# Attention stage of a graph network: VectorE's wide products read a bank operand, GpSimd adds the own rows, three sum banks

## The chip, the cores and the metric

One core of one Trainium2 chip. The metric is the device time of the whole kernel in microseconds (us); an execution's own time stands beside the span that the hardware profiler gives for it.

## The reference

Four layers of a graph network on 50,000 nodes with 64 features and 50,000 edges, sorted by their destination node. Each layer is `x = x + layer(relu(layernorm(x)))`: a convolution, a mean, an attention layer and a layer with two edge types that runs three times. The change touches the attention layer, with 4 heads:

```python
src, dst = edges + one loop per node
m = leaky_relu(x_l[src] + x_r[dst] + e_emb, 0.2)      # (edges, 4, 64)
alpha = einsum('ehf,hf->eh', m, att)
amax = segment_max(alpha, dst); ex = exp(alpha - amax[dst])
denom = segment_sum(ex, dst)
out = segment_sum(x_l[src] * (ex / (denom[dst] + 1e-16)), dst)
out = batch_norm(out.mean(axis=heads) + bias), then relu
```

## The kernel before

The kernel runs stage after stage: preparation, the two first layers (`norm_layer`), `edge_rows` (scores of the edges), `segment_max`, `attention`, `batch_norm`, and `typed_layer` three times. All data is float32. Scores and their largest values per node are there when `attention` (L2465) begins; it makes the weighted sums, projects them to the outputs and gathers the moments for `batch_norm`.

**Tiles and steps.** `attention` goes over the nodes in NS = 56 steps of HS = 7 tiles of 128 nodes. Since the edges are sorted, the edges of a step lie in a window of WT = 8 tiles of 128 edges. Per step n:

- SyncE's queue (`load`, `store`): the window of edge rows `win` (issue L2515), the exponentials of the edges into the last 8 columns of `M` (L2518), the 7 tiles of the nodes' own rows `own` (L2522); the outputs of an earlier step to memory (L2528). Each load waits until its buffer, one of two, is read: `win` for the messages, the exponentials for the sums, `own` for the products with it.
- VectorE: `matrices` (L2693), 14 matrices of 128x128 that are 1 where an edge's node is the column's node (`S`, from `node_id` and `edge_id`); `messages` (L2700), edge rows times the exponentials of the 4 heads, into `M` (tiles 0 to 4); GpSimd makes tiles 5 to 7 (L2552).
- TensorE: `sums` (L2582), for each tile of nodes two matmuls of `S` with `M` (264 columns) into one of four banks in turn. ScalarE copies each to `agg` (`take`, L2633).
- VectorE: `differences` (L2706, L2708, L2710, L2711) and, after ScalarE's `exps` (L2624), `weights` (L2716, L2718, L2720, L2722): small instructions on 28 elements a partition that join the loop edge's share to the softmax. L2722 writes `cc`, the factors of the sums and those of the own rows.
- VectorE: `scale` (L2737), `agg` times its factors. ScalarE (L2642, tiles 0 to 2, one activation for each tile and head) and GpSimd (L2559, tiles 3 to 6) make `mine`, the own rows times theirs. VectorE adds `mine` to `agg` (L2743, L2745).
- TensorE: `turns` (L2595) transposes `agg` through banks 4 to 6, ScalarE copies (`turned`, L2652); `outputs` (L2604) projects into bank 7, ScalarE copies (L2659); VectorE takes the `moments` (L2728, bn_stats).

**Order.** Each engine has one list, written out by hand. The lists of a step n, with earlier and later steps interleaved:

```python
# VectorE                      # ScalarE                       # TensorE
differences(n)                 take(n, 0, 2)                   sums(n, 0, 4)
matrices(n + 2)                own_edges(n - 1, 0, 1)          outputs(n - 2)
weights(n)                     take(n, 2, 4)                   sums(n, 4, 7)
scale(n)                       own_edges(n - 1, 1, 3)          turns(n - 1)
messages(n + 2)                outputs(n - 2)                  # GpSimd
add(n)                         take(n, 4, 7)                   own_edges(n)
moments(n - 2)                 turned(n - 1, 0, 2); exps(n)    messages(n + 2)
                               turned(n - 1, 2, 4)             # SyncE: store(n - 2), load(n + 2)
```

Elsewhere in the kernel: the stages of the typed and the first layers make the same matrices with the ids in a bank (L2360) and messages with a factor in a bank (L2143). In `batch_norm`, VectorE's L2877 reads a bank and SBUF while GpSimd's L2822 works on two SBUF operands.

Of the kernel before, what the change touches and what calls it, by code (L numbers as in the profile page):

```python
# [27 lines left out]
def build_gnn(nc, a, out):  # L28
# [47 lines left out]
    with ctx:  # L76
# [2388 lines left out]
        def attention(tag):  # L2465
            with nc.cleanup_on_exit(), ExitStack() as c, nc.Block() as block:
# [5 lines left out]
                OWN_ACT, MSG_DVE = 3, 5  # L2472
                taken = [0]

                def carve(buf, shape):
# [9 lines left out]
                den = carve(early, [P, 2, HS, HEADS]); d = carve(early, [P, 2, HS, HEADS]); cc = carve(early, [P, 2, HS, HEADS])  # L2485
# [7 lines left out]
                (shift_in, S_ok, M_ok, M2_ok, sums_ok, taken_ok, d_ok, e_ok, c_ok, mine_ok, mine2_ok, agg_ok, aT_made, aT_read, out_made, o_ok, stat_ok, turned_stats, var_ok, sd_ok) = (  # L2493
                    sm(n) for n in ("shift_in", "S_ok", "M_ok", "M2_ok", "sums_ok", "taken_ok", "d_ok", "e_ok", "c_ok", "mine_ok", "mine2_ok", "agg_ok", "aT_made", "aT_read", "out_made",
# [3 lines left out]
                SPLIT_AT = 4  # L2498
# [4 lines left out]
                @block.sync  # L2503
                def _(sp):
                    for half in range(2):
                        sp.dma_start(shift[half * F:(half + 1) * F, :], o_col[:, :]).then_inc(shift_in, 16)

                    def load(n):
                        s = n % 2
                        begin = nc.sync.value_load(starts[0:1, n:n + 1], min_val=0, max_val=FRONT + NP)  # L2510
                        at = slice(n * HS * P, (n + 1) * HS * P)
                        if n >= 2:
                            sp.wait_ge(M_ok, n - 1)
                            sp.wait_ge(M2_ok, n - 1)
                        sp.dma_start(win[:, s, :, :], tiles(edge_all[bass.ds(begin, WR), :])).then_inc(win_in[s], 16)  # L2515
                        if n >= 2:
                            sp.wait_ge(sums_ok, HS * (n - 1))
                        sp.dma_start(M[:, s, :, HF:MW], tiles(exp_all[bass.ds(begin, WR), :])).then_inc(ex_in[s], 16)  # L2518
                        if n >= 2:
                            sp.wait_ge(mine_ok, n - 1)  # L2520
                            sp.wait_ge(mine2_ok, n - 1)
                        sp.dma_start(own[:, s, :, :], tiles(node_g[at, :])).then_inc(own_in[s], 16)  # L2522

                    def store(n):
                        sp.wait_ge(o_ok, n + 1)
                        for half in range(2):
                            lo = n * HS * P + half * HALF
                            sp.dma_start(gat_rows[:, lo:lo + HALF], oT[half * F:(half + 1) * F, n % 2, :]).then_inc(stored[n % 2], 16)  # L2528
                    load(0)
                    load(1)  # L2530
                    for n in range(NS):
                        if n >= 2:
                            store(n - 2)
                        if n + 2 < NS:
                            load(n + 2)
                    store(NS - 2)
                    store(NS - 1)
                    sp.wait_ge(stat_ok, NS)
                    sp.dma_start(stats[0:F, NS:2 * NS, :], stats[F:2 * F, 0:NS, :]).then_inc(turned_stats, 16)
                    for s in range(2):  # L2540
                        sp.wait_ge(stored[s], 16 * NS)

                @block.gpsimd
                def _(pool):
                    g = nc.gpsimd

                    def messages(n):
                        s = n % 2
                        pool.wait_ge(win_in[s], 16 * (n // 2 + 1))
                        pool.wait_ge(ex_in[s], 16 * (n // 2 + 1))  # L2550
                        k = WT - MSG_DVE
                        g.tensor_tensor(heads(M[:, s, MSG_DVE:WT, 0:HF]), win[:, s, MSG_DVE:WT, :].unsqueeze(2).to_broadcast((P, k, HEADS, F)),  # L2552
                                        M[:, s, MSG_DVE:WT, HF:HF + HEADS].unsqueeze(3).to_broadcast((P, k, HEADS, F)), ALU.mult).then_inc(M2_ok, 1)

                    def own_edges(n):
                        s, k = n % 2, HS - OWN_ACT
                        pool.wait_ge(c_ok, n + 1)
                        pool.wait_ge(own_in[s], 16 * (n // 2 + 1))
                        g.tensor_tensor(mine[:, OWN_ACT:HS, :, :], own[:, s, OWN_ACT:HS, :].unsqueeze(2).to_broadcast((P, k, HEADS, F)),  # L2559
                                        cc[:, 1, OWN_ACT:HS, :].unsqueeze(3).to_broadcast((P, k, HEADS, F)), ALU.mult).then_inc(mine2_ok, 1)  # L2560

                    messages(0)
                    messages(1)
                    for n in range(NS):
                        own_edges(n)
                        if n + 2 < NS:
                            messages(n + 2)

                @block.tensor
                def _(pe):  # L2570
                    def sums(n, t0, t1):
                        s = n % 2
                        if t0 == 0:
                            pe.wait_ge(S_ok, n + 1)
                            pe.wait_ge(M_ok, n + 1)
                            pe.wait_ge(M2_ok, n + 1)
                        for t in range(t0, t1):
                            g = n * HS + t
                            if g >= 4:
                                pe.wait_ge(taken_ok, g - 3)  # L2580
                            for q in range(BAND):
                                ins = nc.tensor.matmul(bank[g % 4][:, 0:MW], S[:, s, BAND * t + q, :], M[:, s, t + q, :], start=(q == 0), stop=(q == BAND - 1))  # L2582
                            ins.then_inc(sums_ok, 1)

                    def turns(n):
                        s = n % 2
                        pe.wait_ge(agg_ok, n + 1)
                        for k, (b, q, to) in enumerate(TURNS):
                            if k == 3:
                                pe.wait_ge(aT_read, 4 * n + 1)  # L2590
                            elif n >= 1 and k == 0:
                                pe.wait_ge(aT_read, 4 * n)
# [26 lines left out]
                def _(act):  # L2619
# [6 lines left out]
                    def take(n, t0, t1):  # L2626
# [3 lines left out]
                        for t in range(t0, t1):  # L2630
                            g = n * HS + t
                            act.wait_ge(sums_ok, g + 1)
                            A.copy(agg[:, s, t, :], bank[g % 4][:, 0:MW]).then_inc(taken_ok, 1)  # L2633

                    def own_edges(n, t0, t1):
                        s = n % 2
                        if t0 == 0:
                            act.wait_ge(c_ok, n + 1)
                            act.wait_ge(own_in[s], 16 * (n // 2 + 1))
                        for t in range(t0, t1):  # L2640
                            for h in range(HEADS):
                                ins = A.activation(mine[:, t, h, :], own[:, s, t, :], ACT.Copy, scale=cc[:, 1, t, h:h + 1])  # L2642
                        if t1 == OWN_ACT:
                            ins.then_inc(mine_ok, 1)
# [17 lines left out]
                    for n in range(NS):  # L2662
                        take(n, 0, 2)
                        if n >= 1:
                            own_edges(n - 1, 0, 1)
                        take(n, 2, SPLIT_AT)
                        if n >= 1:
                            own_edges(n - 1, 1, OWN_ACT)
# [8 lines left out]
                    own_edges(NS - 1, 0, 1)  # L2677
                    own_edges(NS - 1, 1, OWN_ACT)
# [7 lines left out]
                def _(dve):  # L2686
                    v = nc.vector

                    def matrices(n):
# [3 lines left out]
                        v.tensor_tensor(S[:, s, :, :], node_id[:, :].unsqueeze(1).to_broadcast((P, BAND * HS, P)),  # L2693
                                        edge_id[:, n * BAND * HS:(n + 1) * BAND * HS].unsqueeze(2).to_broadcast((P, BAND * HS, P)), ALU.is_equal).then_inc(S_ok, 1)

                    def messages(n):
# [3 lines left out]
                        v.tensor_tensor(heads(M[:, s, 0:MSG_DVE, 0:HF]), win[:, s, 0:MSG_DVE, :].unsqueeze(2).to_broadcast((P, MSG_DVE, HEADS, F)),  # L2700
                                        M[:, s, 0:MSG_DVE, HF:HF + HEADS].unsqueeze(3).to_broadcast((P, MSG_DVE, HEADS, F)), ALU.mult).then_inc(M_ok, 1)
# [11 lines left out]
                    def weights(n):  # L2713
# [8 lines left out]
                        v.tensor_tensor(cc[:, :, :, :], d[:, :, :, :], den[:, 0:1, :, :].to_broadcast((P, 2, HS, HEADS)), ALU.mult).then_inc(c_ok, 1)  # L2722
# [12 lines left out]
                    def scale(n):  # L2735
                        s = n % 2
                        v.tensor_tensor(heads(agg[:, s, :, 0:HF]), heads(agg[:, s, :, 0:HF]), cc[:, 0, :, :].unsqueeze(3).to_broadcast((P, HS, HEADS, F)), ALU.mult)  # L2737

                    def add(n):
                        s = n % 2  # L2740
                        v.drain()
                        dve.wait_ge(mine_ok, n + 1)
                        v.tensor_tensor(heads(agg[:, s, 0:OWN_ACT, 0:HF]), heads(agg[:, s, 0:OWN_ACT, 0:HF]), mine[:, 0:OWN_ACT, :, :], ALU.add)  # L2743
                        dve.wait_ge(mine2_ok, n + 1)
                        v.tensor_tensor(heads(agg[:, s, OWN_ACT:HS, 0:HF]), heads(agg[:, s, OWN_ACT:HS, 0:HF]), mine[:, OWN_ACT:HS, :, :], ALU.add).then_inc(agg_ok, 1)  # L2745

# [4 lines left out]
                    for n in range(NS):  # L2751
# [7 lines left out]
                        add(n)  # L2759
# [206 lines left out]
```

## Time and profile before

| | us |
|---|---|
| median of 3 runs (5031.31 to 5033.49) | 5033.35 |
| profiled execution, its own time | 5037.59 |
| its span | 5035.3 |
| busy: PE, DVE, ACT, POOL | 3799.1, 3579.0, 2050.9, 2845.2 |
| attention stage, first matrices to last moments | 2512.7 to 3270.5 |

PE is TensorE, DVE VectorE, ACT ScalarE, POOL GpSimd, SP SyncE. A row of the timeline gives the start and the length of an instruction, or of several alike that follow each other (x4), its engine, line, operation, `out<-in` by the names of the buffers, and in brackets how long the engine was idle before it and what ended that. Buffers that share memory carry the name of the memory: `early` holds `M`, `own`, `cc` and the small ones, `alpha` holds `win`; `famine` is `mine`, `faagg` is `agg`. A PEclk of 1.00 is TensorE's full clock.

### The profile page before, as it was taken

The page shows a single profiled execution, that of the slowest core. Times are in us where ns is not written, and L with a number is a line of the kernel's source. Part 1 is how long each engine was busy: PE and PEld are TensorE (multiplying, and loading weights), DVE is VectorE, ACT ScalarE, POOL GpSimd, SP SyncE. Part 2 cuts the span into 40 slices and gives each one's busy share as a digit, 9 for nine tenths or more (in the row PEclk, how much of TensorE's full clock was granted, in tenths as well). Part 3 has the DMA queues.
Part 4 walks back from the last instruction along what each step waited for, and adds up shares of the span by engine and source line. Part 5 has one row for each costly group of instructions (what it writes and reads, how often), then busy time and mean ns, then how long its engine had stood idle before and what let it go on. Part 6 is the DMA issues. An engine that isn't in the chain of part 4 may idle for free. (4 is left out here: it accounts for less than half of the span.)

```text
span 5035.3 us, 82559 instructions
## 1 busy us (share of the span) xinstructions
PE 3799.1 (75%) x25394; PEld 3408.4 (68%) x25450; DVE 3579.0 (71%) x8214; ACT 2050.9 (41%) x5050; POOL 2845.2 (57%) x2918
## 2 busy tenths in 40 slices
PE   5710577748887999999378888796888688868888
PEld 5710566748786777777255656596888688868887
DVE  8977578757776999999689999885444344434554
ACT  6836244434444444444155656553222122212222
POOL 0011677747775777777033434335777577757775
PEclk9965677778887999999689999955988788888888
DMA  8013578757775444444122222254666456645664
GB/s 218 12 35 79 143 180 192 183 118 158 160 161 122 118 118 115 118 116 118 34 56 61 55 61 55 52 140 120 136 137 135 102 135 136 136 107 131 134 136 110
DMA packets 1646953, 582.97 MB, mean 116 GB/s; under 512 B 1549591, under 2 KB 1583254, under 8 KB 1646298
## 3 DMA queue, kind: packets, MB, share of 16 engines
q1 hardware_dynamic: 925878, 297.74, 26.0%
q10 hardware_dynamic: 636612, 195.74, 16.7%
q0 software_dynamic: 84064, 84.64, 7.6%
q8 instruction: 193, 3.16, 0.3%
q14 instruction: 206, 1.69, 0.1%
HBM read 381.77 MB, written 209.21 MB: 117 GB/s over the span
## 5 line engine op out<-in xcount | busy, mean ns | idle before, releaser
L2001 POOL DMA_INDIRECT early<-node_g,src_w x1173 | 1113.9, 950 | 427.9 <-issue 356.6
L2218 POOL DMA_INDIRECT early<-node_g,src_w x782 | 758.1, 969 | 298.9 <-issue 248.8
L1116 POOL DMA_INDIRECT fscat<-node_g,early x392 | 371.2, 947 | 194.4 <-issue 109.9
L2582 PE MATMUL bank<-early,faS 128*128 128x264 f32 x1568 | 394.0, 406 | 80.7 <-POOL early L2552 80.4
L2582 PEld LDWEIGHTS bank<-early,faS 128*128 128x128 f32 x1568 | 306.1, 201 | 169.7 <-issue 118.6
L1220 ACT ACTIVATE fsy<-bank 128x512 f32<-128x512 f32 x448 | 240.2, 544 | 379.4 <-DVE fslz L1265 201.3
L2262 PE MATMUL bank<-l0S,l0msg 128*128 128x128 f32 x1568 | 271.1, 352 | 157.1 <-issue 62.2
L2262 PEld LDWEIGHTS bank<-l0S,l0msg 128*128 128x128 f32 x1568 | 261.2, 264 | 164.1 <-issue 104.1
L2559 POOL TENSOR_TENSOR famine<-early 128x1024 f32<-128x1024 f32 x56 | 106.5, 1903 | 452.5 <-DVE early L2722 452.5
L2043 PE MATMUL bank<-l3S,l3msg 128*128 128x128 f32 x1568 | 230.6, 316 | 104.4 <-issue 63.6
L2043 PE MATMUL bank<-l5S,l5msg 128*128 128x128 f32 x1568 | 231.1, 316 | 102.3 <-issue 67.8
L2043 PE MATMUL bank<-l4S,l4msg 128*128 128x128 f32 x1568 | 236.5, 321 | 91.8 <-issue 58.7
L2043 PEld LDWEIGHTS bank<-l3S,l3msg 128*128 128x128 f32 x1568 | 221.9, 229 | 108.6 <-issue 108.6
L2043 PEld LDWEIGHTS bank<-l5S,l5msg 128*128 128x128 f32 x1568 | 222.6, 230 | 106.2 <-issue 106.1
L2043 PEld LDWEIGHTS bank<-l4S,l4msg 128*128 128x128 f32 x1568 | 227.7, 234 | 95.7 <-issue 95.7
L1265 DVE TENSOR_TENSOR fslz<-bank,fsy 128x512 f32<-128x512 f32 x448 | 258.3, 618 | 34.8 <-ACT fsy L1220 15.8
L2259 PE MATMUL bank<-ident,l1own 128*64 128x128 f32 x784 | 184.8, 333 | 123.2 <-issue 73.0
L2262 PE MATMUL bank<-l1S,l1msg 128*64 128x128 f32 x1568 | 270.4, 301 | 0.0
L2143 DVE TENSOR_TENSOR l3msg<-early,bank 128x512 f32<-128x512 f32 x112 | 71.9, 683 | 271.5 <-DMA early<-edge_h 271.4
L2143 DVE TENSOR_TENSOR l4msg<-early,bank 128x512 f32<-128x512 f32 x112 | 71.9, 683 | 271.4 <-DMA early<-edge_h 271.2
L1119 POOL DMA_INDIRECT fscat<-node_g,early x224 | 212.0, 947 | 68.3 <-issue 67.7
L2552 POOL TENSOR_TENSOR early<-alpha,early 128x768 f32<-128x768 f32 x56 | 181.6, 3243 | 113.0 <-DMA early<-edge_x 112.9
(368 smaller groups left out, 10820.5 us busy)
## 6 DMA issues: line engine op xcount, KB each, us to landing
edge_h<-early SPq DMA_DIRECT2D x280, 224.0 KB
node_g<-amax ACTq DMA_DIRECT2D x224, 224.0 KB
early<-edge_h SPq DMA_DIRECT2D x168, 256.0 KB
early<-node_g,src_w POOLq DMA_INDIRECT x1955
l0msg<-edge_a ACTq DMA_DIRECT2D x56, 256.0 KB
l0msg<-edge_h SPq DMA_DIRECT2D x56, 256.0 KB
l1msg<-edge_h SPq DMA_DIRECT2D x56, 256.0 KB
alpha<-edge_h SPq DMA_DIRECT2D x56, 256.0 KB
```

What stands on the lines that cost most here:

```text
L1116: pool.indirect_dma_start(out=cat[:, s, t, 0:F], out_offset=None, in_=node_g, in_offset=bass.IndirectOffsetOnAxis(ap=src_i[:, col], axis=0 ...
L1119: pool.indirect_dma_start(out=cat[:, s, t, F:2 * F], out_offset=None, in_=node_g, in_offset=bass.IndirectOffsetOnAxis(ap=dst_i[:, col], ax ...
L1220: A.activation(y[:, g % 2, 0:t1 - t0, :], z_bank(g)[:, 0:(t1 - t0) * HF].rearrange("p (t c) -> p t c", c=HF), ACT.Copy, scale=SLOPE).then_ ...
L1265: v.tensor_tensor(lz[:, kind, t0:t1, :], z_bank(g)[:, 0:(t1 - t0) * HF].rearrange("p (t c) -> p t c", c=HF), y[:, g % 2, 0:t1 - t0, :], AL ...
L2001: pool.indirect_dma_start(out=ring[:, n % RING, t, :], out_offset=None, in_=table_in, in_offset=bass.IndirectOffsetOnAxis(ap=src_w[:, n * ...
L2043: nc.tensor.matmul(to, msg[:, s, t + q, :], S[:, s, BAND * t + q, :], start=(q == 0), stop=(q == BAND - 1))
L2143: ins = v.tensor_tensor(msg[:, n % 2, :, r * F:(r + 1) * F], win[:, n % DEEP, :, :], rel_ps(n)[:, r, :].unsqueeze(2).to_broadcast((P, WT, ...
L2218: pool.indirect_dma_start(out=ring[:, n % RING, t, :], out_offset=None, in_=table_in, in_offset=bass.IndirectOffsetOnAxis(ap=src_w[:, n * ...
L2259: nc.tensor.matmul(bank[2 * s + b][F:2 * F, col], own[:, d, t, :], ident[:, :], start=True, stop=True)
L2262: ins = nc.tensor.matmul(to, msg[:, d, t + q, :], S[:, s, BAND * t + q, :], start=(q == 0 and conv), stop=(q == BAND - 1))
L2552: g.tensor_tensor(heads(M[:, s, MSG_DVE:WT, 0:HF]), win[:, s, MSG_DVE:WT, :].unsqueeze(2).to_broadcast((P, k, HEADS, F)), M[:, s, MSG_DVE: ...
L2582: ins = nc.tensor.matmul(bank[g % 4][:, 0:MW], S[:, s, BAND * t + q, :], M[:, s, t + q, :], start=(q == 0), stop=(q == BAND - 1))
```

## The change

The ids of the nodes, the exponentials of a window (two slots) and the factors of the sums go into bank 3, which the sums give up (a ring of three). VectorE's `matrices`, `messages` and `scale` then read one operand from that bank and one from SBUF. VectorE makes all 8 tiles of messages; `scale` is two instructions, of 4 and 3 tiles. ScalarE makes the own rows of tiles 3 to 6, GpSimd those of tiles 0 to 2; GpSimd adds them, in two parts, and TensorE's `turns` begins with the first part. The factors of the own rows get one buffer, `own_c`, and a wait for its readers.

```diff
-                OWN_ACT, MSG_DVE = 3, 5
+                OWN_POOL = 3
...
-                SPLIT_AT = 4
+                SPLIT_AT, RING = 4, 3
+                ids = bank[3][:, 0:P]
+                ex_ps = lambda n: bank[3][:, P + n % 2 * WT * HEADS:P + (n % 2 + 1) * WT * HEADS].rearrange("p (t h) -> p t h", h=HEADS)
+                sum_c = bank[3][:, P + 2 * WT * HEADS:P + 2 * WT * HEADS + HS * HEADS].rearrange("p (t h) -> p t h", h=HEADS)
...
-                            sp.wait_ge(M2_ok, n - 1)
...
-                            sp.wait_ge(mine_ok, n - 1)
+                            sp.wait_ge(mine_ok, 2 * (n - 1))
...
-                    def messages(n):
+                    def own_edges(n):
                         s = n % 2
-                        pool.wait_ge(win_in[s], 16 * (n // 2 + 1))
-                        pool.wait_ge(ex_in[s], 16 * (n // 2 + 1))
-                        k = WT - MSG_DVE
-                        g.tensor_tensor(heads(M[:, s, MSG_DVE:WT, 0:HF]), win[:, s, MSG_DVE:WT, :].unsqueeze(2).to_broadcast((P, k, HEADS, F)),
-                                        M[:, s, MSG_DVE:WT, HF:HF + HEADS].unsqueeze(3).to_broadcast((P, k, HEADS, F)), ALU.mult).then_inc(M2_ok, 1)
-
-                    def own_edges(n):
-                        s, k = n % 2, HS - OWN_ACT
                         pool.wait_ge(c_ok, n + 1)
                         pool.wait_ge(own_in[s], 16 * (n // 2 + 1))
-                        g.tensor_tensor(mine[:, OWN_ACT:HS, :, :], own[:, s, OWN_ACT:HS, :].unsqueeze(2).to_broadcast((P, k, HEADS, F)),
-                                        cc[:, 1, OWN_ACT:HS, :].unsqueeze(3).to_broadcast((P, k, HEADS, F)), ALU.mult).then_inc(mine2_ok, 1)
-
-                    messages(0)
-                    messages(1)
+                        pool.drain()
+                        g.tensor_tensor(mine[:, 0:OWN_POOL, :, :], own[:, s, 0:OWN_POOL, :].unsqueeze(2).to_broadcast((P, OWN_POOL, HEADS, F)),
+                                        own_c[:, 0:OWN_POOL, :].unsqueeze(3).to_broadcast((P, OWN_POOL, HEADS, F)), ALU.mult).then_inc(mine2_ok, 1)
+
+                    def add(n, b):
+                        s, (t0, t1) = n % 2, CH[b]
+                        pool.wait_ge(scaled, 2 * n + b + 1)
+                        pool.wait_ge(mine_ok, 2 * n + b + 1)
+                        pool.drain()
+                        g.tensor_tensor(heads(agg[:, s, t0:t1, 0:HF]), heads(agg[:, s, t0:t1, 0:HF]), mine[:, t0:t1, :, :], ALU.add).then_inc(agg_ok, 1)
+
                     for n in range(NS):
                         own_edges(n)
-                        if n + 2 < NS:
-                            messages(n + 2)
+                        add(n, 0)
+                        add(n, 1)
...
-                            if g >= 4:
-                                pe.wait_ge(taken_ok, g - 3)
+                            if g >= RING:
+                                pe.wait_ge(taken_ok, g - RING + 1)
                             for q in range(BAND):
-                                ins = nc.tensor.matmul(bank[g % 4][:, 0:MW], S[:, s, BAND * t + q, :], M[:, s, t + q, :], start=(q == 0), stop=(q == BAND - 1))
+                                ins = nc.tensor.matmul(bank[g % RING][:, 0:MW], S[:, s, BAND * t + q, :], M[:, s, t + q, :], start=(q == 0), stop=(q == BAND - 1))
                             ins.then_inc(sums_ok, 1)
 
                     def turns(n):
                         s = n % 2
-                        pe.wait_ge(agg_ok, n + 1)
                         for k, (b, q, to) in enumerate(TURNS):
+                            if q == 0:
+                                pe.wait_ge(agg_ok, 2 * n + b + 1)
...
-                        if t0 == 0:
+                        if t0 == OWN_POOL:
                             act.wait_ge(c_ok, n + 1)
                             act.wait_ge(own_in[s], 16 * (n // 2 + 1))
+                            if n >= 1:
+                                act.wait_ge(agg_ok, 2 * n)
                         for t in range(t0, t1):
                             for h in range(HEADS):
-                                ins = A.activation(mine[:, t, h, :], own[:, s, t, :], ACT.Copy, scale=cc[:, 1, t, h:h + 1])
-                        if t1 == OWN_ACT:
-                            ins.then_inc(mine_ok, 1)
+                                ins = A.activation(mine[:, t, h, :], own[:, s, t, :], ACT.Copy, scale=own_c[:, t, h:h + 1])
+                        ins.then_inc(mine_ok, 1)
...
-                            own_edges(n - 1, 0, 1)
+                            own_edges(n - 1, OWN_POOL, SPLIT_AT)
                         take(n, 2, SPLIT_AT)
                         if n >= 1:
-                            own_edges(n - 1, 1, OWN_ACT)
+                            own_edges(n - 1, SPLIT_AT, HS)
...
-                        v.tensor_tensor(S[:, s, :, :], node_id[:, :].unsqueeze(1).to_broadcast((P, BAND * HS, P)),
+                        v.tensor_tensor(S[:, s, :, :], ids.unsqueeze(1).to_broadcast((P, BAND * HS, P)),
                                         edge_id[:, n * BAND * HS:(n + 1) * BAND * HS].unsqueeze(2).to_broadcast((P, BAND * HS, P)), ALU.is_equal).then_inc(S_ok, 1)
 
                     def messages(n):
                         s = n % 2
                         dve.wait_ge(win_in[s], 16 * (n // 2 + 1))
                         dve.wait_ge(ex_in[s], 16 * (n // 2 + 1))
-                        v.tensor_tensor(heads(M[:, s, 0:MSG_DVE, 0:HF]), win[:, s, 0:MSG_DVE, :].unsqueeze(2).to_broadcast((P, MSG_DVE, HEADS, F)),
-                                        M[:, s, 0:MSG_DVE, HF:HF + HEADS].unsqueeze(3).to_broadcast((P, MSG_DVE, HEADS, F)), ALU.mult).then_inc(M_ok, 1)
+                        v.tensor_copy(ex_ps(n), M[:, s, :, HF:HF + HEADS])
+                        v.drain()
+                        v.tensor_tensor(heads(M[:, s, :, 0:HF]), win[:, s, :, :].unsqueeze(2).to_broadcast((P, WT, HEADS, F)),
+                                        ex_ps(n).unsqueeze(3).to_broadcast((P, WT, HEADS, F)), ALU.mult).then_inc(M_ok, 1)
 
                     def differences(n):
                         s, tl = n % 2, slice(n * HS, (n + 1) * HS)
...
                         v.drain()
                         v.reciprocal(den[:, 0, :, :], den[:, 1, :, :])
                         v.drain()
-                        v.tensor_tensor(cc[:, :, :, :], d[:, :, :, :], den[:, 0:1, :, :].to_broadcast((P, 2, HS, HEADS)), ALU.mult).then_inc(c_ok, 1)
+                        if n >= 1:
+                            dve.wait_ge(mine_ok, 2 * n)
+                            dve.wait_ge(mine2_ok, n)
+                        v.tensor_tensor(own_c[:, :, :], d[:, 1, :, :], den[:, 0, :, :], ALU.mult).then_inc(c_ok, 1)
+                        v.tensor_tensor(sum_c, d[:, 0, :, :], den[:, 0, :, :], ALU.mult)
                         v.drain()
 
                     def moments(n):
...
 
                     def scale(n):
                         s = n % 2
-                        v.tensor_tensor(heads(agg[:, s, :, 0:HF]), heads(agg[:, s, :, 0:HF]), cc[:, 0, :, :].unsqueeze(3).to_broadcast((P, HS, HEADS, F)), ALU.mult)
-
-                    def add(n):
-                        s = n % 2
-                        v.drain()
-                        dve.wait_ge(mine_ok, n + 1)
-                        v.tensor_tensor(heads(agg[:, s, 0:OWN_ACT, 0:HF]), heads(agg[:, s, 0:OWN_ACT, 0:HF]), mine[:, 0:OWN_ACT, :, :], ALU.add)
-                        dve.wait_ge(mine2_ok, n + 1)
-                        v.tensor_tensor(heads(agg[:, s, OWN_ACT:HS, 0:HF]), heads(agg[:, s, OWN_ACT:HS, 0:HF]), mine[:, OWN_ACT:HS, :, :], ALU.add).then_inc(agg_ok, 1)
-
+                        for t0, t1 in CH:
+                            v.tensor_tensor(heads(agg[:, s, t0:t1, 0:HF]), heads(agg[:, s, t0:t1, 0:HF]), sum_c[:, t0:t1, :].unsqueeze(3).to_broadcast((P, t1 - t0, HEADS, F)), ALU.mult).then_inc(scaled, 1)
+
+                    v.tensor_copy(ids, node_id[:, :])
+                    v.drain()
                     matrices(0)
                     messages(0)
                     matrices(1)
...
                         scale(n)
                         if n + 2 < NS:
                             messages(n + 2)
-                        add(n)
                         if n >= 2:
                             moments(n - 2)
                     moments(NS - 2)
```

## Rows read from the trace of the kernel before

**Rows 1.** Busy us (count) of PE, PEld, DVE, ACT, POOL; clock, DMA share, GB/s.

```profile
2600.00:3200.00 600.00, 489.00 (x2277) 356.09 (x2276) 568.22 (x634) 359.97 (x1143) 235.18 (x92) 0.93 0.27 58
```

**Rows 2.** Timeline of one step: start, length, engine, line; VectorE and GpSimd.

```profile
2702.17 0.19 DVE L2706 TENSOR_TENSOR early<-faagg,no_edge 128x28 f32<-128x28 f32 x1
...
2702.90 2.02 DVE L2693 TENSOR_TENSOR faS<-node_id,edge_id 128x1792 f32<-128x1792 f32 x1
...
2705.75 0.22 DVE L2722 TENSOR_TENSOR early<-early 128x56 f32<-128x56 f32 x1
...
2706.05 1.90 POOL L2559 TENSOR_TENSOR famine<-early 128x1024 f32<-128x1024 f32 x1 [8.07 <-DVE early L2722]
2706.06 3.77 DVE L2737 TENSOR_TENSOR faagg<-faagg,early 128x1792 f32<-128x1792 f32 x1
...
2707.91 3.25 POOL L2552 TENSOR_TENSOR early<-alpha,early 128x768 f32<-128x768 f32 x1
...
2709.75 2.76 DVE L2700 TENSOR_TENSOR early<-alpha,early 128x1280 f32<-128x1280 f32 x1
...
2712.60 0.96 DVE L2743 TENSOR_TENSOR faagg<-faagg,famine 128x768 f32<-128x768 f32 x1
...
2713.48 1.22 DVE L2745 TENSOR_TENSOR faagg<-faagg,famine 128x1024 f32<-128x1024 f32 x1
2714.61 0.62 DVE L2728 BATCH_NORM_STATS2 fastats<-faoT 128x6 f32<-128x448 f32 x1
...
2715.35 0.19 DVE L2706 TENSOR_TENSOR early<-faagg,no_edge 128x28 f32<-128x28 f32 x1
```

**Rows 3.** Timeline of the first step of the stage, VectorE and GpSimd.

```profile
2519.66 1.49 DVE L2700 TENSOR_TENSOR early<-alpha,early 128x1280 f32<-128x1280 f32 x1 [4.93 <-DMA early<-edge_x]
2519.71 5.99 POOL L2552 TENSOR_TENSOR early<-alpha,early 128x768 f32<-128x768 f32 x2 [112.92 <-DMA early<-edge_x]
2521.07 3.29 DVE L2693 TENSOR_TENSOR faS<-node_id,edge_id 128x1792 f32<-128x1792 f32 x1
```

**Rows 4.** Groups by line: count, busy us, mean ns; VectorE with a bank operand.

```profile
L2360 DVE TENSOR_TENSOR l0S<-bank,edge_id 128x1792 f32<-128x1792 f32 x56 | 112.9, 2017 | 0.2
...
L2143 DVE TENSOR_TENSOR l4msg<-early,bank 128x512 f32<-128x512 f32 x112 | 71.9, 683 | 271.4 <-DMA early<-edge_h 271.2 <-issue 0.2
```

**Rows 5.** Timeline of the batch norm stage, VectorE beside GpSimd.

```profile
3330.14 0.62 DVE L2877 SCALAR_TENSOR_TENSOR x_sb<-bank,x_sb 128x448 f32<-128x448 f32 x1
3330.26 0.40 POOL L2822 TENSOR_TENSOR fbt_c<-x_sb,fbln 128x128 f32<-128x128 f32 x1 [1.36 <-DVE fbln L2898]
```

**Rows 6.** Timeline of the step of rows 2, ScalarE.

```profile
2706.00 1.06 ACT L2642 ACTIVATE famine<-early 128x64 f32<-128x64 f32 x4 [0.36 <-DVE early L2722]
...
2706.97 0.63 ACT L2633 COPY faagg<-bank 128x264 f32<-128x264 f32 x2
...
2707.50 2.02 ACT L2642 ACTIVATE famine<-early 128x64 f32<-128x64 f32 x8
...
2709.43 0.62 ACT L2659 ACTIVATE faoT<-bank,fashift 128x448 f32<-128x448 f32 x1
```

**Rows 7.** Timeline of TensorE in one step; busy times of that stretch.

```profile
2557.02 1.88 PE L2595 MATMUL bank<-ident,faagg 128*128 128x128 f32 x14 [1.31 <-DVE faagg L2745]
2558.73 3.73 PE L2582 MATMUL bank<-early,faS 128*128 128x264 f32 x16
...
2564.04 2.94 PE L2582 MATMUL bank<-early,faS 128*128 128x264 f32 x12
...
2557.00:2569.40 12.40, 9.96 (x50) 7.10 (x50) 11.85 (x14) 7.83 (x25) 5.11 (x2) 1.00 0.33 72
```

**Rows 8.** Timeline of the step of rows 2, queue of SyncE.

```profile
2709.55 0.38 SPq L2522 DMA_DIRECT2D early<-node_g  x1
...
2712.77 0.44 SPq L2518 DMA_DIRECT2D early<-edge_x  x1
```

**Rows 9.** The load of the exponentials, L2518: from issue to landing.

```profile
DMA to landing us min/median/max: 2.2/2.8/3.6
```

More of the change, by code:

```diff
@@ L2484, in attention @@
                 me = carve(early, [P, HS, HEADS]); mm = carve(early, [P, HS, HEADS])
-                den = carve(early, [P, 2, HS, HEADS]); d = carve(early, [P, 2, HS, HEADS]); cc = carve(early, [P, 2, HS, HEADS])
+                den = carve(early, [P, 2, HS, HEADS]); d = carve(early, [P, 2, HS, HEADS]); own_c = carve(early, [P, HS, HEADS])
                 win = lent(alpha, 2 * WT * F, lambda shape: tb("win", shape))
@@ L2492, in attention @@
                 win_in, ex_in, own_in, stored = two("win_in"), two("ex_in"), two("own_in"), two("stored")
-                (shift_in, S_ok, M_ok, M2_ok, sums_ok, taken_ok, d_ok, e_ok, c_ok, mine_ok, mine2_ok, agg_ok, aT_made, aT_read, out_made, o_ok, stat_ok, turned_stats, var_ok, sd_ok) = (
-                    sm(n) for n in ("shift_in", "S_ok", "M_ok", "M2_ok", "sums_ok", "taken_ok", "d_ok", "e_ok", "c_ok", "mine_ok", "mine2_ok", "agg_ok", "aT_made", "aT_read", "out_made",
+                (shift_in, S_ok, M_ok, sums_ok, taken_ok, d_ok, e_ok, c_ok, mine_ok, mine2_ok, scaled, agg_ok, aT_made, aT_read, out_made, o_ok, stat_ok, turned_stats, var_ok, sd_ok) = (
+                    sm(n) for n in ("shift_in", "S_ok", "M_ok", "sums_ok", "taken_ok", "d_ok", "e_ok", "c_ok", "mine_ok", "mine2_ok", "scaled", "agg_ok", "aT_made", "aT_read", "out_made",
                                     "o_ok", "stat_ok", "turned_stats", "var_ok", "sd_ok"))
@@ L2575, in sums @@
                             pe.wait_ge(M_ok, n + 1)
-                            pe.wait_ge(M2_ok, n + 1)
                         for t in range(t0, t1):
                             g = n * HS + t
-                            if g >= 4:
-                                pe.wait_ge(taken_ok, g - 3)
+                            if g >= RING:
+                                pe.wait_ge(taken_ok, g - RING + 1)
                             for q in range(BAND):
-                                ins = nc.tensor.matmul(bank[g % 4][:, 0:MW], S[:, s, BAND * t + q, :], M[:, s, t + q, :], start=(q == 0), stop=(q == BAND - 1))
+                                ins = nc.tensor.matmul(bank[g % RING][:, 0:MW], S[:, s, BAND * t + q, :], M[:, s, t + q, :], start=(q == 0), stop=(q == BAND - 1))
                             ins.then_inc(sums_ok, 1)
@@ L2632, in take @@
                             act.wait_ge(sums_ok, g + 1)
-                            A.copy(agg[:, s, t, :], bank[g % 4][:, 0:MW]).then_inc(taken_ok, 1)
+                            A.copy(agg[:, s, t, :], bank[g % RING][:, 0:MW]).then_inc(taken_ok, 1)
                     def own_edges(n, t0, t1):
                         s = n % 2
-                        if t0 == 0:
+                        if t0 == OWN_POOL:
                             act.wait_ge(c_ok, n + 1)
                             act.wait_ge(own_in[s], 16 * (n // 2 + 1))
+                            if n >= 1:
+                                act.wait_ge(agg_ok, 2 * n)
                         for t in range(t0, t1):
                             for h in range(HEADS):
-                                ins = A.activation(mine[:, t, h, :], own[:, s, t, :], ACT.Copy, scale=cc[:, 1, t, h:h + 1])
-                        if t1 == OWN_ACT:
-                            ins.then_inc(mine_ok, 1)
+                                ins = A.activation(mine[:, t, h, :], own[:, s, t, :], ACT.Copy, scale=own_c[:, t, h:h + 1])
+                        ins.then_inc(mine_ok, 1)
                     def turned(n, k0, k1):
@@ L2676, in _ @@
                             turned(n - 1, 2, 4)
-                    own_edges(NS - 1, 0, 1)
-                    own_edges(NS - 1, 1, OWN_ACT)
+                    own_edges(NS - 1, OWN_POOL, SPLIT_AT)
+                    own_edges(NS - 1, SPLIT_AT, HS)
                     outputs(NS - 2)
```

## The prediction

> **What bounds the kernel now.** I read the page first: the stages follow one another, so the change can pay only inside the attention stage, and I left the page's chain alone (it follows the last stage). The busy times of 2600 to 3200 us show which engine sets the pace there [rows 1]: VectorE is busy 568 of 600 us, TensorE 489 at a granted clock of 0.93, ScalarE 360, GpSimd 235. Then the timeline of one step [rows 2]: from one L2706 to the next are 13.18 us (2702.17 to 2715.35), and VectorE's instructions stand end to end. Start to start: differences 0.73, matrices and weights 3.16, scale 3.69, messages 2.85, the two adds 2.01, moments 0.74. That sums to 13.18, so VectorE alone sets the step.
>
> Two of these are longer than their work. The adds give VectorE's pace with no GpSimd work beside it: 768 elements in 0.96 us and 1024 in 1.22, so 1.04 ns an element and some 0.155 us. By that, scale (1792) needs 2.02 us and takes 3.77; messages (1280) need 1.49 and take 2.76. In [rows 2] L2559 starts at 2706.05 on GpSimd and L2737 at 2706.06 on VectorE. GpSimd ends 1.90 us later, and scale ends 1.88 us after that. GpSimd's own messages (L2552) then end 1.33 us after scale, and VectorE's messages 1.35 us after those. Each waits for the one that started first and then runs at its own pace. The stage's first step shows it from the other side [rows 3]: there VectorE's messages came first and took 1.49; the matrices, issued behind GpSimd's messages, took 3.29 in place of 2.02. So each full step loses 3.77 - 2.02 = 1.75 and 2.76 - 1.49 = 1.27, together 3.0 us, to waits for GpSimd.
>
> **One operand from PSUM.** The rows show no price for it: the same matrices with the ids in a bank take 2017 ns, and a product with per-row factors in a bank takes 683 ns for 512 elements (688 by the pace above) [rows 4]. And such an instruction does not wait: in the next stage L2877 (a bank and SBUF) runs its 0.62 us across the whole of GpSimd's L2822, which itself takes 0.40 [rows 5]. So matrices, scale and messages should run at their own pace beside GpSimd.
>
> VectorE's new step: differences 0.73; matrices and weights 3.16 plus 0.05 for one product becoming two; scale as pieces of 1024 and 768, 1.13 + 0.88 = 2.01 by the adds' spacing [rows 2]; the copy of the exponentials to the bank with its drain 0.3 (L2722 is a small instruction of 0.22, and 0.09 lie between its end and L2737); messages for all 8 tiles, 2048 elements, 2.21; adds gone; moments 0.74. Sum 9.2, so 4.0 less than now. The copy of the ids at the head of the stage falls into the 4.93 us in which VectorE waits for the first loads [rows 3].
>
> **What is late next.** With VectorE at 9.2 three other loops are near.
>
> TensorE: in steps at a granted clock of 1.00, turns to sums take 1.71 us, four tiles of sums and the outputs 5.31, three tiles 2.8 (three quarters of the four's 3.73) to 2.94 [rows 7], so 9.8 to 10.0 if it never waits. The three-bank ring costs nothing: a tile waits for the copy of the tile three before it, and ScalarE copies tiles 0 to 3 ahead of its long block of own rows.
>
> ScalarE with VectorE: own rows on ScalarE go from 12 activations to 16. From the weights to the last copy of the next step's sums ScalarE has four activations 0.97, two copies 0.53, then eight 1.93 [rows 6] which become twelve, 2.9, outputs 0.6, three copies 0.95: 5.95 us. Then VectorE needs differences, matrices and weights up to own_c, 2705.75 + 0.18 - 2702.17 = 3.76 [rows 2]. With 0.1 of hand-overs that is 9.8 a step. The new wait of own_c for both kinds of own rows holds nothing up: ScalarE's lie ahead of the copies for which the differences wait, GpSimd's end 8 us earlier.
>
> GpSimd: its pace is 1.90 us for 1024 [rows 2] and 0.40 for 128 [rows 5], so 1.7 ns an element and 0.18. Own rows (768) 1.45, the add of four tiles 1.9, of three 1.5, with drains of 0.1: 5.1 a step, no bound by itself. But the second add waits for ScalarE's twelve activations, 0.1 + 0.97 + 0.53 + 2.9 = 4.5 us after the weights, and ends at 6.2 or so, while the differences want to start at 6.0. These small instructions still have two SBUF operands, so the first waits 0.2 behind the add, as scale does now. The step becomes 9.8 + 0.2 = **10.0 us**. No row has an add of two full streams on GpSimd. From below, 1.5 ns an element gives no wait, 9.8; from above, the 3.25 us of L2552, if all of it were GpSimd's own work, gives 4.2 ns. I take 1.7, because L2559 is nearest in form and L2552 shows the same pace once scale is out of its way (1.33 us for 768).
>
> The Trainium skill (SBUF — State Buffer, "Who interferes with whom") says that a VectorE instruction with two SBUF inputs contends with a GpSimd instruction that reads SBUF, the later one being blocked to the end of the first. By that rule every small instruction that meets an add waits, which speaks against putting the adds on GpSimd; without it the step would be 9.8 and the gain 183 us. The Trainium skill (GPSIMD Engine Reference, "Performance versus the Vector engine") gives 4497 ns for an add of 2048 elements, by estimate 2.2 ns an element; the second add would end 0.4 us later, the step be 10.4 and the gain 150.
>
> Loads: SP starts the load of the exponentials 3.2 us after that of the own rows, and issuing it takes 0.44 [rows 8]; it lands 2.2 to 3.6 us after issue, mostly 2.8 [rows 9]. The own rows' load can go 4.5 us into a step, so the exponentials are there at 4.5 + 3.7 + 2.8 = 11.0, at worst 11.8; VectorE asks for them in the next step, at 10.0 + 2.1 = 12.1. The slack of 0.3 to 1.1 us covers it, but it is thin: behind that wait stand the moments and the next differences, and ScalarE's exponentials wait for these.
>
> **The sum.** 54 of the 56 steps have matrices and messages ahead. 54 x (13.18 - 10.0) = 172 us. I count nothing for the last two and for the head. The profiled execution would take 5037.6 - 172 = 4865.6; the median of the runs lies 4.2 under the profiled time, so **4861 us**.
>
> **Rivals.**
> A, a late partner: the gain is there, but the step is 10.6 to 11.2 us, because loads miss their slack by 1 us, because adds run at 2.8 ns (10.9 by the chain under C), or because TensorE, then nearly the longest loop, is granted 0.9 (9.8 / 0.9 = 10.9). For it: four loops within 1 us of each other, and the present 0.93; against: the clock was full in the steps of [rows 7], where TensorE waited more than it would. At 11.0, 54 x 2.18 = 118, so 4915 us.
>
> B, the change doesn't do what it says: a bank operand does not free VectorE from GpSimd. Scale waits for own rows, the first add for scale, messages for that add, the second add for messages, differences for the second add: 0.1 + 1.45 + 2.0 + 1.9 + 2.2 + 1.5 + 3.8 = 12.95 us, so 54 x 0.23 = 12 gained, 5021 us. Against it stands the overlap of [rows 5], though with only 128 elements on GpSimd.
>
> C, slower: GpSimd's adds become the bound. Its chain is own rows, first add, second add, then VectorE from differences to own_c: 0.1 + 1.45 + 0.1 + (1.024r + 0.18) + 0.1 + (0.768r + 0.18) + 0.05 + 3.76 = 5.92 + 1.79r, with r in ns an element. From r = 4.05 on it is longer than 13.18. The pace that L2552 would have if its 3.25 us were its own, 4.2, gives 13.45 us, 54 x 0.27 = 15 more, 5048 us. For it: L2552 writes rows of 264 elements, which the adds both read and write, with a second full stream besides; against: L2552 ends a constant 1.33 us after scale, and the first two, met by shorter VectorE instructions, took 5.99 together and not 6.5 [rows 3].
>
> **How the numbers follow.** A difference under 0.2% (10 us) can't be told from none. Forecast (step 9.6 to 10.5) 0.73; A 0.16; B 0.03; C 0.05; a mixture of B or C that ends within 10 us of now 0.03. Faster is the forecast with A and B, 0.92; same 0.03; slower 0.05. Low end: TensorE a little under its rows, 9.6, 54 x 3.58 = 193, so 4840. High end: nearly all of A, 11.2, 54 x 1.98 = 107, so 4926; I put 4925. That leaves out B, C and the tails, under 2 in 10.
>
> **What would show it.** Right: scale as 1.22 and 0.96 us and messages as 2.29 on VectorE with GpSimd busy beside them; matrices 2.02 throughout; 10 us from one first difference to the next, which is itself longer than 0.19 behind the second add; TensorE busy over 0.9 of the stage at a clock near 1.0; the stage some 170 us shorter, the others unchanged. Wrong: a three-tile add much over 1.5 us (A or C), scale pieces lengthened by a GpSimd instruction (B), the exponentials' copy waiting for its load or a granted clock near 0.9 (A).

## The result

The changed kernel takes 4875.41 us by the median of its runs (4873.93 to 4877.39), the kernel before beside it 5032.33; the ratio is 0.9688, interval 0.9677 to 0.9700. That is 157 us, where 172 were forecast; the time lies in the range. The profiled execution took 4874.43 us over a span of 4872.4.

The gain is in the steps: the instruction that hands the factors of the own rows on (L2722 before, L2728 after) starts first and last at 2535.3 and 3256.0 us before, at 2533.7 and 3097.3 after, so 13.10 and 10.25 us a step over 55 steps. 55 x 2.85 = 157.

Busy times of the changed kernel from 2600 to 3000 us, columns as in [rows 1]:

```profile
2600.00:3000.00 400.00, 382.00 (x1944) 278.76 (x1943) 352.66 (x586) 333.14 (x1126) 219.60 (x117) 1.00 0.34 75
```

TensorE is busy 382 of 400 us at full clock, VectorE, which was busy 95% of the time, 353. One step of the timeline, as in [rows 2] and [rows 6]:

```profile
2702.54 1.82 POOL L2562 TENSOR_TENSOR faagg<-faagg,famine 128x768 f32<-128x768 f32 x1 [0.58 <-ACT famine L2644]
...
2703.68 0.72 DVE L2709 TENSOR_TENSOR early<-faagg,no_edge 128x28 f32<-128x28 f32 x1 [0.61 <-ACT faagg L2633]
...
2704.94 2.02 DVE L2694 TENSOR_TENSOR faS<-bank,edge_id 128x1792 f32<-128x1792 f32 x1
...
2707.86 0.19 DVE L2728 TENSOR_TENSOR early<-early 128x28 f32<-128x28 f32 x1
...
2708.09 1.06 ACT L2644 ACTIVATE famine<-early 128x64 f32<-128x64 f32 x4 [0.60 <-DVE early L2728]
2708.21 1.47 POOL L2554 TENSOR_TENSOR famine<-early 128x768 f32<-128x768 f32 x1 [3.86 <-DVE early L2728]
2708.23 2.08 DVE L2745 TENSOR_TENSOR faagg<-faagg,bank 128x1024 f32<-128x1024 f32 x2
...
2709.06 0.63 ACT L2633 COPY faagg<-bank 128x264 f32<-128x264 f32 x2
...
2709.59 2.98 ACT L2644 ACTIVATE famine<-early 128x64 f32<-128x64 f32 x12
2709.85 2.37 POOL L2562 TENSOR_TENSOR faagg<-faagg,famine 128x1024 f32<-128x1024 f32 x1 [0.16 <-issue]
...
2710.49 2.29 DVE L2703 TENSOR_TENSOR early<-alpha,bank 128x2048 f32<-128x2048 f32 x1
2712.47 0.61 ACT L2660 ACTIVATE faoT<-bank,fashift 128x448 f32<-128x448 f32 x1
...
2712.79 1.82 POOL L2562 TENSOR_TENSOR faagg<-faagg,famine 128x768 f32<-128x768 f32 x1 [0.58 <-ACT famine L2644]
2712.98 0.91 ACT L2633 COPY faagg<-bank 128x264 f32<-128x264 f32 x3
...
2713.93 0.72 DVE L2709 TENSOR_TENSOR early<-faagg,no_edge 128x28 f32<-128x28 f32 x1 [0.61 <-ACT faagg L2633]
...
2714.66 0.88 PE L2595 MATMUL bank<-ident,faagg 128*128 128x128 f32 x6 [0.42 <-POOL faagg L2562]
...
2718.11 0.19 DVE L2728 TENSOR_TENSOR early<-early 128x28 f32<-128x28 f32 x1
```

The two pieces of scale (L2745) take 2.08 us beside GpSimd's 1.47, messages for 8 tiles (L2703) 2.29 across the add. The wide instructions of [rows 2] that waited for GpSimd wait no more. The 56 matrices take 2014 to 2026 ns, and all messages keep their pace too (shortest, median, longest in ns, first and last start):

```profile
L2703 DVE TENSOR_TENSOR early<-alpha,bank x56: 2286/2287/2289, 2518.2 to 3081.4; 128x2048 f32<-128x2048 f32 x56
```

What waits now is a small one. GpSimd's second add starts at 2712.79, once ScalarE's twelve activations are done, and takes 1.82; the first difference (L2709) starts at 2713.93 and needs 0.72 in place of 0.19. GpSimd's adds take 2.37 and 1.82, not the 1.9 and 1.5 of the working.

### The profile page after: what moved, and what is told of

Read it like the earlier page. It is cut to its first block and busy times, and to the rows that moved or that the text cites. A ratio compares the mean times of both kernels' runs of the same rounds, so it can differ in the third digit from the quotient of the medians.

```text
span 4872.4 us, 83123 instructions
## 1 busy us (share of the span) xinstructions
PE 3738.3 (77%) x25450; PEld 3357.5 (69%) x25450; DVE 3384.4 (69%) x8271; ACT 2090.5 (43%) x5274; POOL 2879.4 (59%) x2974
## 5 line engine op out<-in xcount | busy, mean ns | idle before, releaser
L2581 PE MATMUL bank<-early,faS 128*128 128x264 f32 x1568 | 375.3, 392 | 79.5 <-DVE early L2703 78.4
L2581 PEld LDWEIGHTS bank<-early,faS 128*128 128x128 f32 x1568 | 290.8, 191 | 163.0 <-issue 79.5
L2554 POOL TENSOR_TENSOR famine<-early 128x768 f32<-128x768 f32 x56 | 82.5, 1474 | 337.7 <-DVE early L2728 337.7
L2562 POOL TENSOR_TENSOR faagg<-faagg,famine 128x1024 f32<-128x1024 f32 x112 | 234.4, 2092 | 42.6 <-ACT famine L2644 32.2
```

What stands on the lines that cost most here:

```text
L2562: g.tensor_tensor(heads(agg[:, s, t0:t1, 0:HF]), heads(agg[:, s, t0:t1, 0:HF]), mine[:, t0:t1, :, :], ALU.add).then_inc(agg_ok, 1)
L2581: ins = nc.tensor.matmul(bank[g % RING][:, 0:MW], S[:, s, BAND * t + q, :], M[:, s, t + q, :], start=(q == 0), stop=(q == BAND - 1))
```

## Experiments

The diffs are shortened, and an edit of several lines can stand in one. The name of each run stands in brackets.

**The small wait** (e1_diff_bank). Differences with a bank operand too; the copies run while VectorE waits for ScalarE.

```diff
+                        v.tensor_copy(none_ps, no_edge[:, tl])
+                        v.tensor_copy(amax_ps, amax[:, tl, :])
+                        v.drain()
                         dve.wait_ge(taken_ok, HS * (n + 1))
-   me = agg + no_edge; mm = max(me, amax); d0 = me - mm; d1 = amax - mm
+   me = agg + none_ps; mm_ps = max(me, amax_ps); d0 = me - mm_ps; d1 = amax - mm_ps
```

> The changed kernel, with VectorE's differences also given one operand from bank 3: no_edge and amax of the step are copied there while VectorE waits for ScalarE's last copy, and the running maximum is written there. In the changed kernel the first difference takes 0.72 us in place of 0.19, because it starts behind GpSimd's second add. Theory (that wait lies in the loop that sets the step, 10.25 us): it goes, the first difference takes 0.19, the step becomes 9.75 to 9.9 where TensorE's own loop of 9.8 is met, and the time 4875 - 54 x 0.4 = 4853, within 4846 to 4858. Rival (TensorE, busy 382 of 400 us, already sets the step): the wait goes, another takes its place, the time stays above 4870.

4859.37 us, 0.9647 (0.9631 to 0.9663) of the kernel before on that chip. Its timeline, then its busy times:

```profile
2705.59 0.19 DVE L2735 TENSOR_TENSOR early<-early 128x28 f32<-128x28 f32 x1
...
2710.51 1.81 POOL L2566 TENSOR_TENSOR faagg<-faagg,famine 128x768 f32<-128x768 f32 x1 [0.58 <-ACT famine L2648]
...
2711.79 0.18 DVE L2716 TENSOR_TENSOR early<-faagg,bank 128x28 f32<-128x28 f32 x1 [0.37 <-ACT faagg L2637]
...
2712.38 0.87 PE L2599 MATMUL bank<-ident,faagg 128*128 128x128 f32 x6 [0.17 <-POOL faagg L2566]
...
2715.42 0.19 DVE L2735 TENSOR_TENSOR early<-early 128x28 f32<-128x28 f32 x1
...
2725.42 0.19 DVE L2735 TENSOR_TENSOR early<-early 128x28 f32<-128x28 f32 x1
```

```profile
2600.00:3000.00 400.00, 395.83 (x2016) 289.74 (x2015) 352.53 (x684) 348.90 (x1169) 228.43 (x122) 1.00 0.35 77
```

The first difference (2711.79) takes 0.18 although the second add runs until 2712.32. Steps of 9.83 and 10.0 us follow each other in turn, as from one L2735 to the next here; the mean of the 55 steps is 9.91 (first and last L2735 at 2536.7 and 3081.9). TensorE is busy 396 of 400. The time is just above the range expected: the mean step lies at the upper end of 9.75 to 9.9, and on this chip the kernel before took 5035.91, 3.6 us more than beside the changed kernel. So both kernels ran once more, on one chip (e9_changed_again and e10_diff_bank_again).

> The changed kernel once more, beside e10_diff_bank_again on the same chip. A ratio to the kernel before of 0.968 to 0.970, as in its first runs (0.9688).

> The kernel of e1_diff_bank once more, on the chip of e9_changed_again. Theory (the wait of the first difference was worth 0.4 us of the changed kernel's step): 14 to 22 us below e9_changed_again, by medians. Rival (the first pair of runs differed by the chip): less than 5 us.

4871.00 and 4855.57 us, 15.4 apart; 0.9680 (0.9667 to 0.9693), as expected, and 0.9649 (0.9636 to 0.9662). The theory holds, and this version beats both kernels.

**Bank operands taken back, the split of the work kept** (e2_sbuf_operands).

```diff
-                ids = bank[3][:, 0:P]
+                ids = node_id[:, :]
-                sum_c = bank[3][...]
+                sum_c = tb("sum_c", [P, HS, HEADS])[:, :, :]
-                        v.tensor_copy(ex_ps(n), M[:, s, :, HF:HF + HEADS])
-                        v.drain()
-                                        ex_ps(n).unsqueeze(3)...
+                                        M[:, s, :, HF:HF + HEADS].unsqueeze(3)...
```

> The changed kernel with the three bank operands back in SBUF (ids, exponentials, factors of the sums; no copy of the exponentials), the work split as in the changed kernel. Theory (a VectorE instruction with two SBUF operands and a GpSimd one wait for each other, and the bank operand is what ends that): scale waits for own rows, the adds for scale and messages, differences for the adds; a step of 13 to 14 us, 54 x 2.75 to 3.75 more, 5024 to 5078 us. Rival (the split of the work brings the gain, not the bank): within 10 us of 4875.

5041.31 us, 1.0014 (1.0004 to 1.0024): the whole gain is gone. VectorE and GpSimd in one step:

```profile
2708.68 0.19 DVE L2726 TENSOR_TENSOR early<-early 128x28 f32<-128x28 f32 x1
...
2709.04 2.56 POOL L2554 TENSOR_TENSOR famine<-early 128x768 f32<-128x768 f32 x1 [3.86 <-DVE early L2726]
2709.05 3.37 DVE L2743 TENSOR_TENSOR faagg<-faagg,fasum_c 128x1024 f32<-128x1024 f32 x2
...
2711.76 2.87 POOL L2562 TENSOR_TENSOR faagg<-faagg,famine 128x1024 f32<-128x1024 f32 x1 [0.16 <-issue]
2712.34 4.43 DVE L2701 TENSOR_TENSOR early<-alpha,early 128x2048 f32<-128x2048 f32 x1
...
2714.79 3.65 POOL L2562 TENSOR_TENSOR faagg<-faagg,famine 128x768 f32<-128x768 f32 x1 [0.16 <-issue]
...
2717.43 1.05 DVE L2707 TENSOR_TENSOR early<-faagg,no_edge 128x28 f32<-128x28 f32 x1
...
2719.02 2.02 DVE L2694 TENSOR_TENSOR faS<-node_id,edge_id 128x1792 f32<-128x1792 f32 x1
...
2721.94 0.19 DVE L2726 TENSOR_TENSOR early<-early 128x28 f32<-128x28 f32 x1
```

The step is 13.26 us. Each waits in turn: own rows take 2.56 instead of 1.47, scale 3.37, the first add 2.87, messages 4.43 (they end 2.14 after the add), the second add 3.65, the first difference 1.05. This is nearly rival B's chain, which was priced for a bank that doesn't help: it is what SBUF operands do. (In B scale waits for the own rows; here the own rows wait for scale's first piece, and its second piece for them.) What VectorE gave away came back as waits. The matrices (L2694) don't wait, though their ids are in SBUF again: they took 2.02 before [rows 2], take 2.02 here and 2.02 in the changed kernel, for no GpSimd instruction runs when they start. In these steps the ids in the bank show no gain.

**Bank operands alone, the work split as before** (e3_bank_only; a ring of three, too).

```diff
 kernel before, with
+                SPLIT_AT, RING = 4, 3
+                ids, ex_ps, sum_c in bank[3]
+                        v.tensor_copy(ex_ps(n), M[:, s, 0:MSG_DVE, HF:HF + HEADS])
-   cc = d * den
+   cc[:, 1] = d[:, 1] * den; sum_c = d[:, 0] * den
```

> The kernel before with the bank operands alone: matrices, VectorE's 5 tiles of messages and scale read bank 3, sums use a ring of three, but GpSimd still makes 3 tiles of messages and 4 of own rows and VectorE still adds. Theory (the waits of 3.0 us a step were the loss): 13.18 - 3.0 + 0.25 for the copy and the second product = 10.4 us, VectorE end to end, 5032 - 54 x 2.8 = 4881, within 4870 to 4895, so nearly the whole gain without moving any work. Rival (the moved adds carry the gain, since VectorE loses 2 us of them): above 4940.

4888.81 us, 0.9709 (0.9692 to 0.9725):

```profile
2706.38 1.90 POOL L2562 TENSOR_TENSOR famine<-early 128x1024 f32<-128x1024 f32 x1 [7.13 <-DVE early L2727]
2706.48 2.02 DVE L2743 TENSOR_TENSOR faagg<-faagg,bank 128x1792 f32<-128x1792 f32 x1
...
2708.24 1.47 POOL L2555 TENSOR_TENSOR early<-alpha,early 128x768 f32<-128x768 f32 x1
...
2708.67 1.49 DVE L2705 TENSOR_TENSOR early<-alpha,bank 128x1280 f32<-128x1280 f32 x1
...
2710.25 0.96 DVE L2749 TENSOR_TENSOR faagg<-faagg,famine 128x768 f32<-128x768 f32 x1
...
2711.13 1.22 DVE L2751 TENSOR_TENSOR faagg<-faagg,famine 128x1024 f32<-128x1024 f32 x1
```

Scale at 2.02 and messages at 1.49 across GpSimd's 1.90 and 1.47, the own pace of all four. So the operand alone brings 147 of the 157 to 161 us. Moving the adds and messages adds 0.2 to 0.3%, which these intervals hardly resolve; in the profiles the mean step goes from 10.48 (first and last L2727 at 2537.6 and 3114.2, VectorE end to end) only to 10.25.

**What an add costs on GpSimd** (e4_add_repeated).

```diff
-   agg + mine[:, t0:t1, :, :]
+   agg + amax[:, t0:t1, :].unsqueeze(3).to_broadcast((P, t1 - t0, HEADS, F))
```

> The changed kernel, GpSimd's adds with a second operand that repeats one value 64 times (a constant of the step in place of the own rows, which are left out of the sum), rows of agg and waits as they are. Measured in the changed kernel: 2.37 us for 1024, 1.82 for 768, so 2.15 ns an element, where own rows take 1.7. Theory (a second operand with its own value for each element costs the difference): 1.9 and 1.5 us, the first difference waits 0.2, the step is 9.95, the time 4875 - 54 x 0.3 = 4859. Rival (rows of 264 elements, read and written in place, cost it): 2.37 and 1.82 as before, 4875.

4860.85 us, 0.9649 (0.9633 to 0.9665):

```profile
2707.73 1.90 POOL L2562 TENSOR_TENSOR faagg<-faagg,amax 128x1024 f32<-128x1024 f32 x1 [0.16 <-issue]
...
2710.67 1.47 POOL L2562 TENSOR_TENSOR faagg<-faagg,amax 128x768 f32<-128x768 f32 x1 [1.04 <-ACT famine L2644]
...
2711.81 0.38 DVE L2709 TENSOR_TENSOR early<-faagg,no_edge 128x28 f32<-128x28 f32 x1 [0.60 <-ACT faagg L2633]
```

1.90 and 1.47: with the rows of 264 and the place unchanged, the repeated operand is worth the whole difference, (1.90 - 1.47) / 256 = 1.7 ns an element against (2.37 - 1.82) / 256 = 2.15. The first difference takes 0.38, a wait of 0.2, and the time is the one that was expected with this pace (4859). The mean step is 9.91 (first and last L2728 at 2537.4 and 3082.3).

**The ring** (e5_before_ring3). The kernel before with `bank[g % 3]` for `bank[g % 4]` and the wait to match.

> The kernel before with three banks for the sums in place of four, nothing else. Theory (ScalarE copies the first four tiles ahead of its own rows, so a ring of three never holds TensorE up): the same as before within 0.2%. Rival (TensorE waits for a bank once a step, and VectorE's differences come later): 0.3 us a step or more, 16 us slower.

5034.30 us, 0.9998 (0.9988 to 1.0008). It costs nothing there.

**Is it TensorE?** First in the changed kernel (e8_half_out):

```diff
-                        for q in range(2):
+                        for q in range(1):
```

> The changed kernel with the same half of the projection left out (heads 2 and 3 missing from the output) and nothing else. Theory (its 10.25 us are the loop of ScalarE's own rows and copies, the wait of the first difference behind the second add, and VectorE's way to the weights, in which TensorE has slack): within 8 us of 4875. Rival (TensorE's 9.8 with its waits sets the step): 0.4 us a step less, 4854.

4876.75 us, 0.9680 (0.9664 to 0.9697): no gain.

```profile
2705.98 1.81 POOL L2562 TENSOR_TENSOR faagg<-faagg,famine 128x768 f32<-128x768 f32 x1 [0.58 <-ACT famine L2644]
...
2707.12 0.72 DVE L2709 TENSOR_TENSOR early<-faagg,no_edge 128x28 f32<-128x28 f32 x1 [0.61 <-ACT faagg L2633]
...
2707.85 0.87 PE L2595 MATMUL bank<-ident,faagg 128*128 128x128 f32 x6 [1.17 <-POOL faagg L2562]
```

The time TensorE saves turns up as a longer wait for the second add (1.17 us before the turns, 0.42 in the changed kernel, where this wait, 40 times, makes up all 18.0 us that TensorE is idle between 2600 and 3000). TensorE does not set the changed kernel's step. Then in the version with the bank differences, first with GpSimd taking one tile more (e6_pool_four):

```diff
-                OWN_POOL = 3
+                OWN_POOL = 4
-                            own_edges(n - 1, OWN_POOL, SPLIT_AT)
```

> e1_diff_bank with GpSimd making 4 tiles of own rows and ScalarE 3, so ScalarE has 0.97 us less between the weights and its last copy. In e1_diff_bank the step is 9.83 us and TensorE is busy 396 of 400 us. Theory (TensorE sets the step there): no gain, 4859 within 8 us, or a few us slower since the second add ends 0.2 us later. Rival (ScalarE's own rows and copies with VectorE's differences and weights, 9.7, set it): a step of 9.3 to 9.5, 4834 to 4845.

4860.49 us, 0.9650 (0.9634 to 0.9666): no gain, so ScalarE's share alone doesn't set that step. (The 9.83 in the expectation is the short step of e1_diff_bank; the mean is 9.91.) And with half the projection left out besides (e7_pool_four_half_out):

> e6_pool_four with half of the projection left out (two of four matmuls, heads 2 and 3 missing from the output), so TensorE has 0.8 us less a step. Theory (TensorE sets the step of e6_pool_four): next are VectorE's instructions, 9.2 and two small copies, and the loop through the second add, so 9.4 to 9.5, 54 x 0.4 = 20 us less than e6_pool_four. Rival (something else does): no more than 5 us less.

4854.32 us, 0.9640 (0.9624 to 0.9656), 6 us less where 20 were expected, and hardly more than the rival's 5. Busy times, then TensorE, ScalarE and GpSimd in one step:

```profile
2600.00:3000.00 400.00, 369.90 (x1872) 280.71 (x1871) 356.70 (x690) 312.38 (x1016) 247.14 (x122) 1.00 0.36 78
```

```profile
2702.28 0.38 ACT L2638 COPY faagg<-bank 128x264 f32<-128x264 f32 x1 [0.51 <-PE bank L2586]
...
2705.75 1.82 POOL L2567 TENSOR_TENSOR faagg<-faagg,famine 128x768 f32<-128x768 f32 x1 [0.28 <-ACT famine L2649]
...
2707.63 0.87 PE L2600 MATMUL bank<-ident,faagg 128*128 128x128 f32 x6 [0.75 <-POOL faagg L2567]
...
2712.11 0.38 ACT L2638 COPY faagg<-bank 128x264 f32<-128x264 f32 x1 [0.51 <-PE bank L2586]
2712.38 2.98 ACT L2649 ACTIVATE famine<-early 128x64 f32<-128x64 f32 x12
```

TensorE is busy 370 of 400 us, and the step is 9.83 (copy of the fourth tile at 2702.28 and 2712.11), nearly throughout. In e6_pool_four steps of 10.03 and 9.83 took turns, as in e1_diff_bank (L2732 at 2699.14, 2709.17, 2719.00, 2729.04); with half the projection out the long ones become 9.83 too. That is 0.1 us a step on average, and 55 x 0.1 is nearly all of the 6 us. What holds the step at 9.83 is a closed loop: the turns wait 0.75 us for the second add, the next sums follow them, ScalarE's block of twelve activations starts only behind the copy of the fourth of these tiles (2712.11), and the next second add only behind that block (at 2705.75 it waits 0.28 us for it). I had left ScalarE's block out of that loop. With the whole projection TensorE is idle 4.2 us of 400 in e1_diff_bank and 4.6 in e6_pool_four, 3.4 and 4.6 of them in waits for the second add; for the rest its own work fills these steps. So TensorE leaves the bank-difference version no room as it is, and in e6_pool_four the other loop stands only 6 us behind it. Why long and short steps take turns stays open.

## Why the prediction was right, and where it was off

- *The wide instructions wait for GpSimd, 3.0 us a step, and a bank operand ends it*: right. e2_sbuf_operands brings the waits back with the new split, e3_bank_only removes them with the old.
- *No price for the bank operand*: right, 2.29 for 2048 elements as worked out; the copy of the exponentials (L2701) takes 0.18, with its drain 0.26.
- *VectorE at 9.2 no longer sets the step*: right, it waits 0.61 for ScalarE and is busy 353 of 400.
- *The ring costs nothing, the loads keep their slack*: right. e5_before_ring3 shows the first, and in the changed kernel TensorE waits for the second add alone; no copy of the exponentials waited for its load after the first.
- *The loop through ScalarE, the second add, and the differences sets the step; 9.8 + 0.2*: the loop is right. From the end of the factors (2708.05) the second add starts after 4.74 us (4.5 and hand-overs in the working), the first difference after 5.88 (6.0). The term that was mis-sized is GpSimd's pace in the adds. I took 1.7 ns an element from L2559, whose operands are both repeated, as nearest in form; the add of two full streams takes 2.15. With 1.82 in place of 1.5 the wait is 0.53, not 0.2, and the step 10.25. 54 x 0.25 = 13.5 us, nearly all of the 14 between 4861 and 4875. With adds at 1.7 ns (e4_add_repeated) the wait is the 0.2 of the working and the time 4861. The estimate from the Trainium skill (GPSIMD Engine Reference, "Performance versus the Vector engine"), 2.2 ns, agrees with the 2.15 measured and was the better one: it gave a step of 10.4 and a gain of 150, against 10.25 and 157.
- *Small instructions with two SBUF operands wait behind an add*: right, as the Trainium skill (SBUF — State Buffer, "Who interferes with whom") has it: the first difference takes 0.72 in the changed kernel, and 0.18 in e1_diff_bank, where the operand alone took the wait away.
- *Rivals*: A did not come, TensorE's clock is 1.00 and the loads are in time. B is refuted. C needed 4.05 ns an element; it is 2.15, and L2552's 3.25 us was waiting, as e3_bank_only shows (1.47).

## What to carry to other kernels

Where VectorE and GpSimd work side by side, look for instructions of either that take twice their work: a small, repeated operand copied to a bank ends the wait for less than 0.3 us. Do this to the small instructions as well, once the big ones are done, and look which of them start behind a GpSimd instruction. Price a GpSimd instruction from a row whose operands repeat, or don't, in the same way.

## What was not expected

A GpSimd instruction with a repeated second operand is faster by a fifth than one with two full streams (1.7 against 2.15 ns an element), the other operand, its row length and the place being the same. The loop through the second add and ScalarE's block was not expected either: it holds the step at 9.83 us with half of the projection gone, so 6 us came where 20 were expected.
